# Field-pair projection: three rows of the fifth DMA engine's x gathered apart instead of five rows of two engines, and two rows of one other engine by a second small gather

## What is computed

```python
xi = x[:, pi, :]
xj = x[:, pj, :]
proj = jnp.einsum('bpd,pod->bpo', xi, W)
return proj * xj
```

## Time and profile before

| | us |
|---|---|
| median of 3 runs | 670.62 |
| lowest, highest | 669.97, 671.05 |
| the profiled execution: its own time | 670.16 |
| its span in the profile | 668.4 |

### The profile page before, as it was taken

The page is one execution under the profiler, slowest core; times in us unless marked ns, Lnnn a source line. Parts: engine busy times, 40 slices in busy tenths (PEclk is TensorE's granted clock), DMA queues, the critical chain, the costliest instruction groups (busy, mean ns, idle before and its releaser), DMA issues.

```text
span 668.4 us, 7464 instructions
## 1 busy us (share of the span) xinstructions
PE 577.2 (86%) x2704; PEld 340.8 (51%) x2704; DVE 410.9 (61%) x528; ACT 232.1 (35%) x301; POOL 419.1 (63%) x256
## 2 busy tenths in 40 slices
PE   5998989989898998979979898898989979799930
PEld 4565555545455554645545455465555645456510
DVE  0776666856566665665856566465666756567630
ACT  2334334343333334333243333233334243433400
POOL 0866848585765866757585774666748575656720
PEclk9999999999999998998999999798999999999975
DMA  8999999999999999999999999999999999999997
GB/s 347 436 437 427 435 422 433 439 429 429 437 429 430 432 433 426 443 433 428 428 431 433 426 432 436 433 427 432 424 428 436 434 429 423 444 423 437 440 424 321
DMA packets 11257, 285.15 MB, mean 427 GB/s; under 512 B 1776, under 2 KB 1904, under 8 KB 2672
## 3 DMA queue, kind: packets, MB, share of 16 engines
q1 hardware_dynamic: 8496, 270.27, 94.1%
q0 software_dynamic: 2464, 14.68, 5.2%
q10 hardware_dynamic: 288, 0.08, 0.1%
HBM read 25.56 MB, written 260.05 MB: 427 GB/s over the span
## 4 chain that ended last, share of the span: by engine, by line
DMA 55%; PE 22%; POOL 7%; DVE 6%; issue 3%; ACT 2%; SPq 0%; DVEq 0%; ACTq 0%; POOLq 0%
DMA out_dram<-staged 37%; PE proj L378 19%; DMA x_in<-x_dram,rows_sb 18%; DVE staged L427 6%; POOL staged L301 6%; PE proj L356 3%; ACT staged L343 2%; DMA ident_sb<-ident_dram 1%; PE proj L400 1%; POOL x_in L283 0%; POOL x_in L274 0%; ACT x_t L328 0%; SPq L248 0%; DVEq L424 0%; ACT x_sb L321 0%
## 5 line engine op out<-in xcount | busy, mean ns | idle before, releaser
L378 PE MATMUL proj<-w_sb,x_t 64*128 64x512 f32 (+7 forms) x2432 | 540.1, 542 | 43.0 <-ACT staged L343 26.8
L427 DVE TENSOR_TENSOR staged<-proj,x_sb 128x1024 f32<-128x1024 f32 (+7 forms) x528 | 410.9, 826 | 231.5 <-PE proj L378 199.9
L301 POOL TENSOR_TENSOR staged<-staged,x_sb 128x1024 f32<-128x1024 f32 (+4 forms) x224 | 390.5, 1756 | 215.3 <-ACT staged L343 211.1
L378 PEld LDWEIGHTS proj<-w_sb,x_t 64*128 64x128 f32 x2432 | 307.9, 190 | 260.0 <-issue 123.8
L343 ACT ACTIVATE staged<-proj 128x1024 f32<-128x1024 f32 (+4 forms) x224 | 171.3, 786 | 323.4 <-PE proj L378 267.0
L321 ACT ACTIVATE x_sb<-x_in 128x2048 f32<-128x2048 f32 x14 | 26.7, 1910 | 68.5 <-DMA x_in<-x_dram,rows_sb 68.5
L356 PE MATMUL proj<-ident_sb,x_sb 128*128 128x128 f32 x256 | 37.1, 292 | 14.3 <-DVE staged L427 14.3
L356 PEld LDWEIGHTS proj<-ident_sb,x_sb 128*128 128x128 f32 x256 | 29.6, 148 | 33.2 <-DVE staged L427 27.3
L328 ACT ACTIVATE x_t<-proj 128x512 f32<-128x512 f32 (+1 forms) x62 | 34.7, 609 | 13.1 <-PE proj L356 13.1
L283 POOL DMA_INDIRECT x_in<-x_dram,rows_sb x14 | 14.5, 1036 | 3.0 <-issue 1.3
L274 POOL DMA_INDIRECT x_in<-x_dram,rows_sb x14 | 13.9, 991 | 2.5 <-issue 2.5
## 6 DMA issues: line engine op xcount, KB each, us to landing
out_dram<-staged SPq DMA_DIRECT2D x16, 5504.0 KB, 24.4
out_dram<-staged SPq DMA_DIRECT2D x15, 5472.0 KB, 24.9
out_dram<-staged SPq DMA_DIRECT2D x16, 4896.0 KB, 25.3
out_dram<-staged SPq DMA_DIRECT2D x1, 3520.0 KB, 16.6
w_sb<-w_dram SPq DMA_DIRECT2D x1, 2944.0 KB, 21.3
out_dram<-staged SPq DMA_DIRECT2D x1, 1952.0 KB, 12.8
w_sb<-w_dram SPq DMA_DIRECT2D x1, 1664.0 KB, 12.1
w_sb<-w_dram SPq DMA_DIRECT2D x1, 1408.0 KB, 14.9
```

The costliest lines, as they stand in the source:

```text
L301: last = nc.gpsimd.tensor_tensor(product, product, x_sb[tile.parity][:, j * dim:(j + n) * dim], ALU.mult)
L378: last = nc.tensor.matmul(proj[b][h][:, at:at + width], x_t[half, turned_at(i, fields), :], w_sb[half, col:col + width], start=True, stop= ...
L427: last = nc.vector.tensor_tensor(staged_part(item, i, j, n), proj[b][h][:, at:at + n * dim], x_sb[tile.parity][:, j * dim:(j + n) * dim], ...
```

## The change

`APART` shrinks from partitions 15 to 19 (one of engine 3, four of engine 4) to 16 to 18 (three of engine 4). A second small gather follows the first on POOL: for tile t it fetches two partitions of another engine, `SPARED[t]`, a different one in each of the tiles 2 to 15. Engines 3 and 4 are not in that list. In the main gather these two partitions are skipped as well. Both small gathers raise `x_apart_loaded` by 16, and the main gather waits for 32 per tile instead of 16. The table of row numbers has three blocks of columns instead of two.

```diff
-APART = range(15, 20)
+APART = range(16, 19)
+
+SPARED = dict(zip(range(2, 16), (8, 9, 10, 11, 12, 13, 14, 15, 0, 1, 2, 5, 6, 7)))
+
+
+def spared_row(number):
+    return 64 * (SPARED[number] // 8) + 4 * (SPARED[number] % 8)
...
-        rows_sb = sb("rows_sb", [P, 2 * tiles], U32)
+        rows_sb = sb("rows_sb", [P, 3 * tiles], U32)
...
                     x_in[APART.start:APART.stop, :], None, x,
                     bass.IndirectOffsetOnAxis(ap=rows_sb[0:len(APART), at:at + 1], axis=0),
                     bounds_check=batch - 1, oob_is_err=False).then_inc(x_apart_loaded, 16)
+                p, at = spared_row(number), 2 * tiles + number
+                nc.gpsimd.indirect_dma_start(
+                    x_in[p:p + 2, :], None, x,
+                    bass.IndirectOffsetOnAxis(ap=rows_sb[0:2, at:at + 1], axis=0),
+                    bounds_check=batch - 1, oob_is_err=False).then_inc(x_apart_loaded, 16)
 
             def load_x(number):
-                pool.wait_ge(x_apart_loaded, 16 * (number - 1))
+                pool.wait_ge(x_apart_loaded, 32 * (number - 1))
...
-    rows = np.full((P, 2 * numbers.shape[1]), NO_ROW, np.uint32)
-    rows[:, :numbers.shape[1]] = numbers
-    rows[APART.start:APART.stop, :numbers.shape[1]] = NO_ROW
-    rows[:len(APART), numbers.shape[1]:] = numbers[APART.start:APART.stop]
+    tiles = numbers.shape[1]
+    rows = np.full((P, 3 * tiles), NO_ROW, np.uint32)
+    rows[:, :tiles] = numbers
+    rows[APART.start:APART.stop, :tiles] = NO_ROW
+    rows[:len(APART), tiles:2 * tiles] = numbers[APART.start:APART.stop]
+    for t in SPARED:
+        spared = slice(spared_row(t), spared_row(t) + 2)
+        rows[spared, t] = NO_ROW
+        rows[:2, 2 * tiles + t] = numbers[spared, t]
```

More of the change, by code:

```diff
@@ L121, in field_pair_project @@
     w_at, w_end = w_columns(fields, dim)
-    assert 2 * dim == P and fields == 32 and tiles % 2 == 0 and tiles >= 4
+    assert 2 * dim == P and fields == 32 and tiles == 16
     assert all(i >= fields // 2 for s in range(TURN_LOW_BEFORE, len(steps)) for unit in steps[s] for i, _, _ in unit)
```

## The result

| kernel | median us | lowest to highest | runs |
|---|---|---|---|
| before | 669.96 | 668.49 to 671.05 | 6 |
| changed | 676.50 | 674.34 to 678.09 | 6 |

The changed kernel is slower: ratio 1.0097, 95% interval 1.0078 to 1.0115, 6.5 us. The forecast was +1.5 us and 672.1, its range ended at 674.4. The direction held, the size didn't. The profiled execution took 677.37 us, span 675.4, so 7.0 us more of span than the one before. One run each of g4 (1,064 us), h3 (1,352 us) and the kernel before (1,064 us) was far slower than all others and is in no number here.

What follows compares the result with a forecast made beforehand. DMA transfers were taken as the bound. Rows on engines 3 and 4 +1.4 us, small packets +0.1, the rest 0: +1.5, so 671.7 us by the profiled execution, 672.1 with the median's 0.46 added; range 668.8 to 674.4.

Steps and rivals of the forecast that it cites:

- The transfers bound the kernel, and the engine with the most to do sets the end: DMA engines: always busy, compute waits for them, so the span ends with the most loaded engine.
- The row price and the two heavier engines: DMA engines 3 and 4: 14 more rows each at 0.31 us; the later one moves the end by +1.4 us.
- the missing early finisher: Engine 4: 17.4 us less row work yet not done early, so its other packets must be 12 to 17 us slower.
- Rival 1: DMA engines 3 and 4 have room and the late two engines get lighter: 670.0 us, chance 0.40.
- The small packets of the second gather: DMA engines: 336 more small packets, 21 per engine, cost 0 to 0.8 us, taken as 0.1.
- POOL's 1 us per issue is covered: POOL: 14 more issues of 0.98 us fit its idle time and cost nothing.
- The wait ahead of the main gather: POOL: in tight tiles x comes 1.0 to 2.6 us later, cost taken as 0; uncovered, up to 36 us.
- The cover: Slot waits of 56.4 + 29.3 us and 12 us of queued stores were to hide the later x.
- Rival 2: Main gather, landing, ACT's copy, next main gather: this loop grows from 38 to 40.5 us and decides; 676 us, chance 0.06.
- Rival 3: Small gathers always begin at the same DMA engines, so two carry 28 extra rows: 674.3 us, chance 0.04.

Runs made afterwards that it cites:

- g4: Changed kernel without its second small gather, the small gather two POOL products earlier and the main gather one earlier: 672.44 us, ratio 1.0046.
- h3: Kernel before with 4,096 instead of 1,024 bytes per partition for the descriptors of POOL's gathers: 669.76 us, ratio 0.9999.
- f4: Kernel before with partitions 14 to 18 apart instead of 15 to 19, in one small gather: 671.86 us, ratio 1.0024.
- f3: Changed kernel with both small gathers two POOL products earlier and the main gather one earlier: 673.95 us, ratio 1.0057.
- g3: f3 with partitions 15 to 19 apart, as before the change, and the two spared rows in the second gather: 673.61 us, ratio 1.0061.
- i1: Kernel before with small gather two products and main gather one product earlier, plus one empty small gather behind the first: 673.77 us, ratio 1.0064.
- f1: Kernel before with an extra 512-column scratch product on POOL straight behind the small gather: 669.93 us, ratio 0.9994.
- f2: Kernel before with an extra 1,024-column scratch product on POOL straight ahead of the main gather: 672.53 us, ratio 1.0039.
- e4: Changed kernel with both small gathers one POOL product step earlier (ahead of item 4 instead of 6): 673.73 us, ratio 1.0041.
- e3: Changed kernel with the main gather one POOL product later (ahead of item 14 instead of 13): 692.78 us, ratio 1.0320.
- e2: Kernel before with its five rows (15 to 19) fetched in two small gathers, of 3 and of 2: 675.21 us, ratio 1.0061.

## Why the prediction was wrong, step by step

- *The transfers bound the kernel, and the engine with the most to do sets the end.* Right in form. But I looked for the loss in the difference between engines, and 6.45 of the 7.0 us of span are common to all of them.
- *The row price and the two heavier engines: +1.4 us.* Right for the rows by themselves. Measured 1.6 us (f4). f4 shows that it is engine 4, whose lighter load only balanced its slower packets, as the argument from the missing early finisher had it. In the packet records of before it ends 2.7 us ahead of the last engine, and 14 x 0.31 - 2.7 = 1.6 us. Rival 1 (room on both) is out. In the changed kernel, beside a second gather, the term may not show at all (f3 and g3 lose the same).
- *The small packets of the second gather: 0 to 0.8 us, taken as 0.1.* **This step failed.** I priced the added transfer by its own packets, and these are as cheap as I had them: 28 more per engine of 9 ns, 0.25 us. But an empty gather costs 4 us (i1), since store packets beside the main gather's rows take longer, 2.0 us per engine in a profiled execution that lost 1.9; no row of before showed a gather with fewer than five rows, so nothing there bounded what it does to others. A range from 0 to 0.8 wasn't a bound on an unknown resource but on its most visible part.
- *POOL's 1 us per issue is covered.* Right (f1).
- *The wait ahead of the main gather: seen, its length of 1 to 2.6 us right (2.66 at 158 us), its cost taken as 0.* **This step failed too**, by 2.3 to 3.1 us (f2, e4). The cover was mis-sized: I subtracted the 13.0 us of a store's own time from its 24.9 us to landing and called 12 us a queue. The rest also holds the x rows in between and the start and end of the transfer. And I named POOL's products behind the wait without asking which store waits for them: it is the second of the tile, issued 0.2 us behind the first of them.
- *Rival 2, the loop.* Its lengths were nearly right (38 us, decides at 40): e3 makes it the bound with one product more. I gave it 0.06 and the price of 676. That price took the tile as 40 us; with the 39.7 us of the earlier trace rows the same sum is 14 x 0.8 = 11 us and not 5.6. In the changed kernel it isn't the steady bound, since slot waits of 72.6 us remain, but it takes the room away that hid the late store.
- *Rival 3* is out: in the packet records of before, the five rows of the small gather fall to five engines, a different set in each tile. The Trainium skill, DMA: Bandwidth & Descriptors, section Why a DMA increments its semaphore by 16 and not by 1, which puts such a gather on as many engines as rows, in turn, agrees.

The parts, each against its own neighbour: 1.6 us for the rows, 4 for a transfer of few rows, 2.3 to 3.1 for the wait, sum 8 to 9, measured 6.5. They aren't independent: e2, with wait and transfer but without the rows, loses 4.1 to 4.9 us, hardly more than i1 with the transfer alone, and f3, with transfer and rows, loses no more than g3 without the rows. With intervals of 1.3 us on each side I can't say how these two share it.

## What to carry to other kernels

When an added transfer is small, its bytes and its issue say little: test it empty, in its place, before counting on what it should bring. Where an engine waits for a transfer in the middle of its list, go one product on from the wait and ask which store that product releases, and read the queue's depth there, in the trace, and not from issue to landing. And where a loop over two engines and a transfer is within a few per cent of the period, an instruction moved by one place can cost more than all that the change was about (e3: 16 us beyond the changed kernel).

## What I hadn't expected of the hardware

- A gather that moves nothing, of two partitions, cost 4 us per run (14 issues, ratio 1.0064); two per tile cost the same. What store packets take longer, they take beside the rows of the main gather, more than 5.7 us behind its issue, and not beside the empty one.
- Rows of 8 KB took 309 ns each beside store packets, and 342.6 ns in the mean of the changed kernel, where the rows ran without stores in some tiles: with all engines on rows, 272 GB/s in place of 430.
- One DMA engine is slower than the others. Followed from end to start through the packet records of before, the one engine with four or five rows per gather, so by its load engine 4, takes 1,478 to 1,495 ns for the 39,168-byte packets, in the mean of a tile, in 14 of the 16, where the others take 1,448 nearly always. From 50 us on its packets take 16.8 us more than at their most frequent lengths, against 15.2 us (49 x 0.31) for the rows that it has less: 59 where the others have 106 to 110, but 95 on the one taken for engine 3. It ended 0.7 us after the median engine. (The Trainium skill, DMA: Bandwidth & Descriptors, section Latency and other measured facts, names engines 7 and 15 as the usually slower ones; here the steadily slow one is another.)
- In the two traces that I followed to their end (before and f4) it is slow only while the compute engines work. In before its last two long packets start at 640.2 and 641.9 us, and the last product of the kernel ends on VectorE at 642.4; from 643.5 us on the packets of this engine take the 1,627 and 1,448 ns of the others. In f4 the last product ends at 646.1 us, the last long packet (1,649 ns) starts at 645.6, and the next, at 647.2, takes 1,627. The last gather had landed some 70 us earlier, so gathers on their way aren't the cause; what is, isn't shown.
- The two engines that ended last in before are other ones, with 110 and 108 rows. Most of their packets have the usual lengths; they are 2.4 and 3.6 us over, 1.7 and 2.3 us of it in 16 single store packets that take 140 to 400 ns too long.
